# Two table buffers instead of one in a rotary embedding, on eight cores

## The reference

```python
# attention part, with X = layernorm(x)
QKV = einsum('bsd,ed->bse', X, W_in) + b_in
Q, K, V = split(QKV, 3, axis=-1)
Q = rope(Q, D // 2); K = rope(K, D // 2)     # rotate the first half of the features
A = sum(feature_map(K) * V, axis=-2)         # feature_map: K over its own norm
Y = einsum('bsd,ed->bse', A[:, None, :] * Q, W_out) + b_out
x = x + (Y + X)
# mixture of 8 experts, with X = layernorm(x): logits, top 2, softmax
x = x + sum_e gates[:, e] * (X @ expert_w[e] + expert_b[e])
```

## Time and profile before

| | us |
|---|---|
| the two runs shown | 2128.18 and 2443.48 (median 2285.83) |
| the profiled execution's own time | 2128.36 |
| its span on the slowest core (core 2) | 2126.8 |
| spans of the other seven cores | 2113.2 to 2126.0 |
| TensorE busy with matmuls | 1673.0 |
| VectorE busy | 654.9 |
| ScalarE, GpSimd busy | 30.5, 69.9 |

### The profile page before, as it was taken

How to read it: one execution, slowest core, us unless ns; L and a number is a source line. 1 busy time by engine, 2 the same in 40 slices (tenths; PEclk the granted TensorE clock), 3 DMA queues, 4 the chain that set the end, 5 groups by cost and what they waited for, 6 DMA issues and landing times.

```text
span 2126.8 us, 19478 instructions; the slowest of 8 cores (2113.2 to 2126.8 us)
## 1 busy us (share of the span) xinstructions
PE 1673.0 (79%) x7766; PEld 773.8 (36%) x7912; DVE 654.9 (31%) x1059; ACT 30.5 (1%) x40; POOL 69.9 (3%) x70
## 2 busy tenths in 40 slices
PE   1498668249966859834964599999999999999994
PEld 1243323124422324421432244444444444444441
DVE  4521133651113342256155222222222222222224
ACT  0000000000000000000001100000000000000000
POOL 0000000000000000000000000000000000000000
PEclk9999889659978879957976699999999999999996
DMA  9242640823165234434522044444444444444424
GB/s 172 81 61 35 94 78 10 173 84 53 29 95 92 50 60 71 73 78 140 80 40 40 1 80 80 80 80 78 73 72 71 72 73 79 80 80 80 80 40 158
DMA packets 132217, 161.78 MB, mean 76 GB/s; under 512 B 6425, under 2 KB 127257, under 8 KB 128033
## 3 DMA queue, kind: packets, MB, share of 16 engines
q0 software_dynamic: 118544, 120.66, 36.3%
q1 hardware_dynamic: 13586, 39.87, 5.6%
HBM read 272.77 MB, written 8.40 MB: 132 GB/s over the span
## 4 chain that ended last, share of the span: by engine, by line
PE 46%; DVE 3%; issue 1%; DMA 1%; DVEq 1%; ACT 1%; ACTq 0%; SPq 0%; POOLq 0%
PE ps_m L892 41%; PE ps_m L680 4%; DVE st L238 1%; PE ps_tr L305 1%; DMA x_scr<-x_all 1%; DVE xln_scr L286 1%; DMA bb_scr<-biases 1%; ACT L780 0%; DVE x L854 0%; DVE x L655 0%; DVE x L650 0%; DVE x2T L313 0%; DVEq L240 0%; PE ps_l L736 0%; DVEq L236 0%
## 5 line engine op out<-in xcount | busy, mean ns | idle before, releaser
L892 PE MATMUL ps_m<-wbuf,x2T 128*128 128x512 bf16 x4014 | 882.4, 380 | 4.7 <-DVE gTb L824 0.5
L417 PE MATMUL ps_m<-wbuf,xlnT 128*128 128x512 bf16 x2507 | 570.7, 389 | 105.9 <-DVE v_sb L429 54.9
L892 PEld LDWEIGHTS ps_m<-wbuf,x2T 128*128 128x128 bf16 x4096 | 401.4, 98 | 485.5 <-issue 4.1
L417 PEld LDWEIGHTS ps_m<-wbuf,xlnT 128*128 128x128 bf16 x2560 | 255.0, 100 | 421.4 <-issue 134.1
L905 DVE SCALAR_TENSOR_TENSOR x<-ps_m,gates,x 128x512 f32<-128x512 f32 x256 | 192.2, 751 | 695.5 <-PE ps_m L892 695.5
L305 PE MATMUL ps_tr<-ident_bf,xln_scr 128*128 128x128 bf16 x384 | 44.8, 309 | 156.1 <-DVE xln_scr L286 156.1
L680 PE MATMUL ps_m<-wbuf,qT 128*128 128x512 bf16 x501 | 117.3, 396 | 39.2 <-DVE x L693 30.2
L429 DVE TENSOR_TENSOR v_sb<-ps_m,bb_scr 128x512 bf16<-128x512 f32 x64 | 43.7, 690 | 208.8 <-PE ps_m L417 208.8
L429 DVE TENSOR_TENSOR k_sb<-ps_m,bb_scr 128x512 bf16<-128x512 f32 x64 | 44.3, 692 | 179.3 <-PE ps_m L417 179.3
L305 PEld LDWEIGHTS ps_tr<-ident_bf,xln_scr 128*128 128x128 bf16 x384 | 39.1, 143 | 161.2 <-issue 161.2
L680 PEld LDWEIGHTS ps_m<-wbuf,qT 128*128 128x128 bf16 x512 | 51.6, 101 | 104.3 <-issue 48.9
(11 more groups left out here) (69 smaller groups left out, 338.8 us busy)
## 6 DMA issues: line engine op xcount, KB each, us to landing
wbuf<-e_w POOLq DMA_DIRECT2D x32, 2048.0 KB, 14.0
x_scr<-x_all SPq DMA_DIRECT2D x24, 1024.0 KB, 5.2
wbuf<-w_kT POOLq DMA_DIRECT2D x8, 2048.0 KB, 23.1
wbuf<-w_vT POOLq DMA_DIRECT2D x8, 2048.0 KB, 18.7
wbuf<-w_qT POOLq DMA_DIRECT2D x4, 2048.0 KB, 14.3
wbuf<-w_oT POOLq DMA_DIRECT2D x4, 2048.0 KB, 14.2
y<-x SPq DMA_DIRECT2D x8, 1024.0 KB, 11.6
bb_scr<-biases POOLq DMA_DIRECT2D x6, 512.0 KB, 7.0
```

Of the source, the lines that this page charges most:

```text
L417: mm = te.matmul(ps[:, :], self.xlnT[:, dc, t * 128:(t + 1) * 128], self.wbuf[q % 2][:, dc, :], start=(dc == 0), stop=(dc == ND - 1))
L892: mm = te.matmul(ps[:, :], self.x2T[:, dc, t * 128:(t + 1) * 128], self.wbuf[si % 2][:, dc, :], start=(dc == 0), stop=(dc == ND - 1))
```

## The change

1. `ct_scr` and `sn_scr` become two buffers each. Tile t uses number t % 2, with a semaphore of its own for each (`self.sct[t % 2]`), and its table load waits for the last rope that used the same pair, which is that of tile t-2.
2. The second layer norm gets its own statistics buffer st2.
3. iota_f becomes float32, a buffer ones_c of one column is added and set to 1 by GpSimd, and the semaphore that released VectorE after the second iota now fires after this memset. No other line uses ones_c.
4. bb_scr is allocated from the right end of the on-chip memory. Most other buffers shift by some hundred bytes to a few KB.

```diff
-        self.iota_f = e(nc.sbuf_tensor("iota_f", [128, 128], BF16))
+        self.iota_f = e(nc.sbuf_tensor("iota_f", [128, 128], F32))
...
+        self.ones_c = e(nc.sbuf_tensor("ones_c", [128, 1], BF16))
...
-        self.st2 = None
-        self.st2 = self.st1
+        self.st2 = e(nc.sbuf_tensor("st2", [128, NTO, 32], F32))
...
-        self.ct_scr = [e(nc.sbuf_tensor("ct0", [128, RH], BF16))] * 2
-        self.sn_scr = [e(nc.sbuf_tensor("sn0", [128, RH], BF16))] * 2
-        self.bb_scr = e(nc.sbuf_tensor("bb_scr", [128, D], BF16))
+        self.ct_scr = [e(nc.sbuf_tensor(f"ct{i}", [128, RH], BF16))
+                       for i in range(2)]
+        self.sn_scr = [e(nc.sbuf_tensor(f"sn{i}", [128, RH], BF16))
+                       for i in range(2)]
+        self.bb_scr = e(nc.sbuf_tensor("bb_scr", [128, D], BF16, side="right"))
...
-                sg.inc(g.iota(self.iota_p[:, :1], [[1, 1]], channel_multiplier=1,
-                              allow_small_or_imprecise_dtypes=True))
+                g.iota(self.iota_p[:, :1], [[1, 1]], channel_multiplier=1,
+                       allow_small_or_imprecise_dtypes=True)
+                sg.inc(g.memset(self.ones_c[:, :], 1.0))
...
-        sct = self.sct[0]
-        ct = self.ct_scr[0]
-        sn = self.sn_scr[0]
+        sct = self.sct[t % 2]
+        ct = self.ct_scr[t % 2]
+        sn = self.sn_scr[t % 2]
...
-            self._wait_free(s, "ct0")
+            self._wait_free(s, f"ct{t % 2}")
...
-        self.free["ct0"] = (sv, sv.n)
+        self.free[f"ct{t % 2}"] = (sv, sv.n)
```

## The result

The changed kernel takes 2083.06 us (median of 11 runs, the lowest 2081.43), the kernel before 2128.81 us (median of 10). The ratio is 0.9774, with a 95% interval of 0.9746 to 0.9801; the two medians by themselves give 0.9785. That the time fell is clear; that it fell by more than 2% is not quite, since the interval reaches across 0.98. Both kernels have single runs far above the rest (up to 2316.87 and 2443.48 us; in the first of these, four cores ran at a mean granted clock of 0.80 to 0.81 and the others at 0.90 to 0.91), which ratios and intervals here leave out and which raise a median by up to 2 us.

The account below looks back on a forecast made before the run. Experts are TensorE alone; in the attention part TensorE waits for VectorE, held by sine-table loads. From 2128.36 us: - 11.6 - 28.7 - 6.8 - 0.7 + 0.2 = -47.6, so 2080.8 us, range 2067 to 2102.

Parts of the forecast that it names:

- the clock term: TensorE after V-quarter stalls: a shorter stall saves 0.15 us of slow clock, five times, 0.7 us in all.
- The table waits go: VectorE's first rope multiplication: waits for the sine table, 40.3 us on K and 7.3 on Q tiles, go except 0.5.
- late pairs: Two K tiles rotated after the last V quarter of each pass: table waits of 6.82 and 4.81 us, 11.6 together, return.
- boundaries: Six places between V-projection quarters, two K tiles rotated at each: 28.7 us of table waits return, TensorE's stalls shrinking equally.
- Q: Ropes of the Q tiles, with transposes between: 6.8 of 7.3 us of table waits come back.
- 4.25 us of stall are left at each boundary: TensorE between V quarters: 10.97 - 6.72 = 4.25 us remains, as two ropes and square-sums outlast two tiles of matmuls.
- The Q stage keeps 0.5 us: Q ropes: table lead 8.3 us against 7.80 or 4.73 seen, so 0.5 us of wait was taken as left over.
- The start costs 0.2 us: Before the first barrier: float32 iota, memset and wider comparison add 0.1 to 0.6 us, taken as 0.2.
- the tile that the prediction called narrow: Q ropes: the table was expected to fit, narrowly for tiles 2 and 3; at 9.1 us each would be 0.8 late.
- only the boundaries: Rival: table waits return only between V quarters, 18.9 us of the waits stay, 2099.7 us; chance 0.12.
- the clock did not stay up: Rival denied here: TensorE's clock stays up through the shorter stalls, six times 2.0, 12 us more gained, 2068.8 us; chance 0.08.
- the slower case: Rival: granted clock gives way in the 880 us expert stretch; a mean under 0.95 uses up the gain; chance 0.06.

Follow-up runs that it names:

- no_tables: The changed kernel with one ct/sn pair again, its four other edits kept: 2129.56 us, ratio 1.0003 to the kernel before.
- tables_only: The kernel before with the second ct/sn pair alone: 2082.82 us, ratio 0.9785 to the kernel before.
- extra_load: The kernel before with a third load of 384 KB, read by nobody, ahead of each pair of table loads: 2165.22 us, ratio 1.0171.
- spread6: The changed kernel with one rope after the fourth and one after the eighth tile of a V quarter, tiles 6 and 7 still late: 2043.54 us, ratio 0.9586.
- k_only: The changed kernel with the second table pair for K tiles only, Q tiles all using pair 0: 2090.11 us, ratio 0.982.

## Why the prediction was right

The forecast was 2080.8 us, the time is 2083.06, inside the range and 2.3 us off. The mechanism was right in its main terms; that the total came so close is in part luck, as the clock term, the one that was not in the sum and the spread of the cores show. In its own steps:

- **The table waits go.** Forecast 11.6 (late pairs) + 28.7 (boundaries) + 6.8 (Q). The waits went as foreseen; the three rope stages gave back 45.5 us in the mean of the cores, whose mean wait was 46.7. Shown by undoing (no_tables), by doing alone (tables_only) and by adding to the wait (extra_load).
- **4.25 us of stall are left at each boundary, 26 us in all.** 4.39 or 4.40 each, 26.4 in all. That it is two ropes in a row against two accumulators is shown by spread6.
- **The Q stage keeps 0.5 us.** 0.4 on the slowest core, 0.6 in the mean; up to 1.4 on core 4, at the tile that the prediction called narrow. Core 4: weights, requests, the first tile's transposes, the second and the third rope:

```profile
856.50 1.14 POOL L374 DMA_DIRECT2D wbuf<-w_oT  x1 [26.48 <-PE ps_m L419]
856.91 0.42 DVE L479 TENSOR_TENSOR tmp<-q_sb,ct 128x512 bf16<-128x512 bf16 x1
...
859.25 0.33 SPq L462 DMA_DIRECT2D ct<-cos_t  x1
...
859.33 1.05 PE L307 MATMUL ps_tr<-ident_bf,q_sb 128*128 128x128 bf16 x16 [3.37 <-DVE q_sb L485]
...
861.42 0.42 DVE L479 TENSOR_TENSOR tmp<-q_sb,ct 128x512 bf16<-128x512 bf16 x1
...
868.05 0.42 DVE L479 TENSOR_TENSOR tmp<-q_sb,ct 128x512 bf16<-128x512 bf16 x1 [1.44 <-DMA sn<-sin_t]
```

  Two readings of the forecast were off here. The request at 859.25 was used at 868.05, after 8.8 us and not the 7.8 read before. And the lead was 8.80 - 1.44 = 7.4 us and not 8.3, because the second rope followed the first after 4.5 us and not 5.3. The first tile's 16 transposes took 1.05 us, at a granted clock of 1.00; in the kernel before they took 1.80, at 0.55:

```profile
898.08 1.80 PE L305 MATMUL ps_tr<-ident_bf,q_sb 128*128 128x128 bf16 x16 [3.38 <-DVE q_sb L483]
```

  k_only shows that the stage is on the path.
- **The clock gives 0.7 us.** This is the term that came out with the wrong sign. The forecast took the shorter stall to save 0.15 us of the dip, five times, from single stalls of one core. Take from the V stages in the mean of the cores their stalls, the wait for the product and 32 tiles at 3.45 us: 8.3 and 8.7 us are left in the kernel before, and 8.3 and 8.7 in the changed one. So the dips stayed whole, and the 0.7 did not come. And the forecast had looked at the clock only behind the six boundaries. At the Q projection, whose work is unchanged, the clock came back later, 1.0 us in the mean. The Trainium skill, page "TensorE: Matmul & The Clock Gate", Part 1, describes a clock that depends on the engine's recent activity. The windows above agree with that; that a shift in one place costs in another is an inference from them, and no run here separates it from other causes.
- **The start costs 0.2 us.** The stage to the first V quarter is 0.2 longer, but it is 223.0 to 223.6 us in other runs with the same start, so that this is no measure of it. The start of the changed kernel, and the comparison before:

```profile
3.39 0.26 POOL L217 IOTA iota_f<- 128x128 f32 x1
...
3.65 0.12 POOL L221 MEMSET ones_c<- 128x1 bf16 x1
3.90 0.29 DVE L226 TENSOR_SCALAR ident_bf<-iota_f,iota_p 128x128 bf16<-128x128 f32 x1 [3.90 <-POOL ones_c L221]
```

```profile
3.85 0.25 DVE L224 TENSOR_SCALAR ident_bf<-iota_f,iota_p 128x128 bf16<-128x128 bf16 x1 [3.85 <-POOL iota_p L218]
```

  The iota is as long with float32 (0.26), the comparison 0.29 instead of 0.25, the memset 0.12. The comparison ends at 4.19 instead of 4.10: the start cost 0.1 us.
- **What was not in the sum:** pass 2 from the product to the first V quarter, +1.8 us. Of it 1.0 is the second wait for V's first weights (20.2 to 21.2 in the mean of the cores, 18 on some cores and 22 on others), about 0.4 the layer norm of pass 2, with waits of 0.3 to 1.0 us for x tiles on some cores. Why the second load of the weights kept TensorE longer was not tested.

The forecast was made for core 2, which was the slowest before. It gained 54.4 us in its span, core 1 only 40.7, against 47.6 forecast. Which core is the slowest changes from execution to execution (core 2 of the changed kernel spans 2072.4 us here and 2083.9 in another run), so one core's gain says little. The mean gain, 43.8 us, and that of the slowest, 45.7, are closer to each other than the cores are, and the forecast is 3.8 and 1.9 us above them.

The rivals: only the boundaries (2099.7) fell with k_only and the wait for the product; the clock did not stay up (2068.8) through stalls of 4.4 us, and did when they went (spread6); the slower case did not come, the expert stretch having the granted clock 1.00 throughout. The 13/16 limit that the same page of the Trainium skill gives for three busy cores of a die is not seen in the profiled executions of the two kernels, in which each of the eight busy cores has the granted clock 1.00 from 1200 to 2000 us.

## What to carry to other kernels

A small table load in a single buffer costs at each use what the work in between does not cover. From request to use it was 2.7 us with no other load under way (requested at 339.90 and used at 342.63 in the kernel before), of which 0.35 were waited, and 9.1 beside a 2 MB weight load, of which 6.72 were; that the weights are the cause was read from the order and not tried. A second buffer made the wait vanish where the request was a quarter ahead, and left up to 1.4 us where it was 7.4 us ahead. But look at the burst that the wait sat in: two ropes with their square-sums in a row, on the engine that has to empty two accumulators, cost 4.4 us and a dip of the clock each time, and spreading them was worth nearly as much as the buffers. And read a queue for what stands behind a waiting DMA: the weights behind the bias row cost 42.5 us, nearly as much as all the table waits.

## What the runs showed that was not expected

- After a stall of 4.4 us the dip of the clock cost 2.05 us (spread6), about as much as after one of 9 to 11 us (2.0 to 2.4 in the rows before). The forecast had this size; what it did not expect is that nothing at all is saved by the shorter stall. Shortening these stalls brought back their length and no more; removing them brought back the dip too.
- Memory addresses and a statistics buffer of its own had no effect that these runs can tell: 2129.56 against 2130.22 us with all of them changed. The forecast had put them at 0.
- The clock moved with the change also where the work did not: it rose later at the Q projection, which took 1.0 us more, and it was still at the fast level in the first Q tile's transposes, which brought the first two ropes closer together and helped to make the third table late. What ties the two together was not tested.
- The load of V's first weights keeps TensorE waiting 18 us on some cores and over 22 on others, in the same execution.
